# Moving the softplus and du arithmetic of a selective-scan kernel from VectorE to ScalarE and GpSimd

## The chip, the cores and the metric

The kernel runs on one core of a Trainium2 chip. The metric is the device time of one launch in microseconds. Five engines work side by side: TensorE (PE; its weight loads are the track PEld), VectorE (DVE), ScalarE (ACT), GpSimd (POOL) and SyncE (SP). Each runs its own instruction list strictly in order; semaphores tie them together.

## What is computed

The input is 16 sequences ("rows") of 512 tokens by 256 features. Each row passes a Mamba-like layer and then a three-layer feed-forward network (FFN), each with a residual and a layer norm. The piece that matters here, cut from the reference, with 512 channels and 16 states:

```
xx = silu(conv1d(x @ in_w.T))                       # u, [channel, time]
delta = softplus(dt @ dt_w.T + dt_b)
dA  = exp(delta * A);  dBu = delta * B * u
carry = dA * carry + dBu;  y = sum_n carry * C      # scan over time, 16 states
y = (y + u * D) * silu(res)
x = layernorm(x + y @ out_w.T); x = layernorm(x + ffn(x))
```

The kernel builds softplus from pieces. With p the pre-activation including its bias, softplus(p) = max(p, 0) + log(1 + exp(-|p|)), plus a correction for what is lost when 1 is added in float32 (the tile that the code keeps in `du` and subtracts).

## The kernel before

**Layout.** Channels lie on partitions, four chunks of 128 (index `c`, `DC` = 4), and time along the free dimension, 512 elements. So "128x512" is one chunk of one row. The scan has 64 tiles per row (16 states by 4 chunks), taken in 32 pairs of 128x1024.

**Pipeline.** One iteration has 64 steps `s`. In it the kernel scans one row, prepares the next one ("front"), finishes the attention part and FFN of the row before ("tail"), and ends the FFN of the one before that ("end"). Every engine walks through the same 64 steps, and tables at the top of the file (`HALF_AT`, `GELU_AT`, `F_DT`, ...) say in which step each piece is issued. The order of each engine is thus written out by hand. An instruction that waits holds up everything behind it on its engine.

**The scan in the steps.** In even steps TensorE transposes a pair of `dB` tiles into `scan_ps` (L367, `b_pair`), for the pair after next but one, once VectorE has emptied those banks. VectorE scans a pair in an even step (L782) and multiplies by C in an odd step into `hC` (L792). GpSimd issues the DMA that adds `hC` to `y2` in odd steps (L968, `y_pair`). `hC` has two buffers: the multiply of pair p waits until the DMA of pair p-2 has landed. ScalarE makes `dA` (L607) and `dB` (L616), several steps ahead.

**The FFN in the steps.** TensorE does half of a hidden tile in each step of `HALF_AT` (L479); steps 51 to 53 have none. ScalarE applies Gelu (L688) and rounds to the high part (L697); GpSimd subtracts for the low part (L990). The half tile of step 55 needs the low parts that GpSimd makes in step 53.

**The stage that is changed**, in the front, for each chunk c:

1. TensorE, steps 41 to 44 (`F_DT`): the pre-activation into `misc_ps` (L423). The matmul of chunk c+1 waits for `dt_ready` of chunk c, since there is one `misc_ps`.
2. VectorE, a step later: adds the bias, `misc_ps` to `delta2` (L818).
3. ScalarE: Abs into `du` (L650), Exp of the negative (L652).
4. VectorE: 1 + e into a work tile `sp_w` (named out_st or gate in the trace, L829), the lost part into `du` (L831), then max(p,0) minus the lost part (L837).
5. ScalarE, step 51: four Ln (L656), with a table load ahead.
6. VectorE, steps 54 and 55: the sum delta (four L843) and du = u * delta (four L848).
7. TensorE, steps 56 to 59 (`F_DU`): transposes `du` into `misc_ps` (L367); the first waits for all four chunks (`du_ready`). ScalarE copies each out (L662), and the next row's `dB` is made from that.
8. VectorE, steps 57 to 60: y2 = D * u (L854), which the first `y_pair` of the next row waits for.

Of the kernel before, what the change touches and what calls it, by code (L numbers as in the profile page):

```python
# [78 lines left out]
F_DT, F_EXP, F_PLUS, F_MAX, F_LN = (41, 42, 43, 44), (43, 44, 45, 48), (44, 45, 46, 49), (45, 46, 47, 50), 51  # L79
F_DELTA, F_DELTA_U, F_Y, F_DU = (54, 54, 55, 55), (54, 54, 55, 55), (57, 58, 59, 60), (56, 57, 58, 59)  # L80
# [14 lines left out]
def build(nc, x, in_wT, chan, xproj_wT, dt_wT, out_wT, ffn_w, ffn_s, w3_s, ident_in, out):  # L95
# [3 lines left out]
    with ExitStack() as ctx:  # L99
# [93 lines left out]
        sp_lost, sp_ln, sp_max = sem("sp_lost"), sem("sp_ln"), sem("sp_max")  # L193
# [387 lines left out]
        def _(act):  # L581
# [37 lines left out]
            def front_step(r, par, s, end):  # L619
# [135 lines left out]
        def _(dve):  # L755
# [40 lines left out]
            def front_step(r, par, s, tail):  # L796
# [36 lines left out]
                for c in range(DC):  # L833
                    if F_MAX[c] != s:
                        continue
                    dve.wait_ge(sp_lost, r * DC + (c + 1))
                    nc.vector.scalar_tensor_tensor(out=delta2[:, par, c, :], in0=delta2[:, par, c, :], scalar=0.0,  # L837
                                                   in1=du[:, c, :], op0=ALU.max, op1=ALU.subtract).then_inc(sp_max, 1)
                for c in range(DC):
                    if F_DELTA[c] == s:  # L840
                        dve.wait_ge(sp_max, r * DC + (c + 1))
                        dve.wait_ge(sp_ln, r * DC + (c + 1))
                        nc.vector.tensor_tensor(delta2[:, par, c, :], delta2[:, par, c, :], sp_w[c], ALU.add  # L843
                                                ).then_inc(delta_ready, 1)
                for c in range(DC):
                    if F_DELTA_U[c] == s:
                        dve.wait_ge(delta_ready, r * DC + (c + 1))
                        nc.vector.tensor_tensor(du[:, c, :], y2[:, par, c, :], delta2[:, par, c, :], ALU.mult  # L848
                                                ).then_inc(du_ready, 1)
                for c in range(DC):  # L850
                    if F_Y[c] != s:
                        continue
                    dve.wait_ge(du_ready, r * DC + (c + 1))
                    nc.vector.tensor_scalar(y2[:, par, c, :], y2[:, par, c, :], ch[:, c, C_D:C_D + 1], None,  # L854
                                            ALU.mult).then_inc(y_init, 1)
# [101 lines left out]
        def _(pool):  # L957
# [11 lines left out]

            def gate_tile(r, par, c):  # L970
# [100 lines left out]
```

## Time and profile before

| what | value |
|---|---|
| median of 3 runs | 3149.71 us (3144.48 to 3151.66) |
| the profiled execution, its time | 3155.72 us |
| its span, first to last instruction | 3153.9 us |
| mean granted TensorE clock | 0.897 |
| TensorE busy | 2583.1 us (82%) |
| VectorE busy | 2621.1 us (83%) |
| ScalarE busy | 2343.3 us (74%) |
| GpSimd busy | 1071.0 us (34%) |

Three engines are busy for three quarters of the span or more. Such a table doesn't say which of them sets the pace in a given stretch: this is read from the chain of waits, which follows the last instruction back through whatever released each step. Times in the traces are microseconds from the start of the span. Line numbers are those of the kernel before. The piece from 1385 to 1568 us is one iteration in the middle; it and its neighbours look alike.

### The profile page before, as it was taken

Reading aid. Unit: us, or ns where it says so; the run is one execution under the profiler, and the core shown is the slowest. Engines: PE = TensorE matmul, PEld = TensorE weight load, DVE = VectorE, ACT = ScalarE, POOL = GpSimd, SP = SyncE. Lnnn points to the kernel's source line nnn. Section 1 sums busy time; section 2 is a strip of 40 time slices with the busy share of each in tenths; the row PEclk is TensorE's granted clock in tenths of the full one; section 3 lists DMA queues with packets and bytes.
Section 4 is the critical chain, followed back from the end, with each engine's and each line's share of the span. In section 5 each row is a group of like instructions: output and inputs, shape, how many; then the busy total and the mean of one; then the engine's idle time right before and its main releaser. Section 6 shows DMA issues by size and latency. Waiting matters only on the chain.

```text
span 3153.9 us, 41504 instructions
## 1 busy us (share of the span) xinstructions
PE 2583.1 (82%) x12290; PEld 1944.8 (62%) x12290; DVE 2621.1 (83%) x2625; ACT 2343.3 (74%) x3653; POOL 1071.0 (34%) x1028
## 2 busy tenths in 40 slices
PE   4355788888888888988888898888888889898888
PEld 1223566676666666676666766666676756666666
DVE  3678998989898897989889898988989898998830
ACT  2776687877969787796968779697877969687822
POOL 0112333333433433343343334234333423423432
PEclk8566899999989999999989999899999989899999
DMA  1996787787878778787887878787787878778933
GB/s 52 290 321 140 167 193 180 185 197 184 194 179 193 190 181 186 183 194 183 190 188 179 194 181 194 179 196 189 178 190 181 200 186 196 189 180 191 229 111 110
DMA packets 230192, 585.49 MB, mean 186 GB/s; under 512 B 26016, under 2 KB 26400, under 8 KB 229808
## 3 DMA queue, kind: packets, MB, share of 16 engines
q0 software_dynamic: 73728, 268.47, 46.2%
q1 hardware_dynamic: 119344, 246.86, 22.4%
q10 hardware_dynamic: 36864, 67.13, 7.9%
q8 instruction: 115, 1.88, 0.2%
q14 instruction: 141, 1.16, 0.1%
HBM read 281.93 MB, written 31.98 MB: 100 GB/s over the span
## 4 chain that ended last, share of the span: by engine, by line
PE 32%; DVE 29%; ACT 17%; issue 14%; DMA 4%; ACTq 1%; DVEq 1%; SPq 1%; POOL 1%; POOLq 0%
PE ffn_ps L479 17%; DVE scan_ps L782 11%; DVE hC L792 5%; PE scan_ps L367 5%; ACT dB L616 4%; ACT dA L607 3%; DVE y L806 3%; PE misc_ps L372 3%; DMA x<-ffn_w 3%; PE misc_ps L423 2%; DVE gate L899 2%; PE misc_ps L460 2%; PE misc_ps L408 2%; ACT L607 2%; PE misc_ps L367 2%
## 5 line engine op out<-in xcount | busy, mean ns | idle before, releaser
L782 DVE TENSOR_TENSOR_SCAN scan_ps<-dA,scan_ps 128x1024 f32<-128x1024 f32 x512 | 1170.8, 2287 | 57.0 <-PE scan_ps L367 33.2
L968 POOL DMA_DIRECT2D y<-hC x512 | 446.1, 871 | 1811.2 <-DVE hC L792 1735.1
L367 PE MATMUL scan_ps<-ident,dB 128*128 128x128 f32 x4096 | 613.4, 300 | 375.7 <-DVE hC L792 292.3
L367 PEld LDWEIGHTS scan_ps<-ident,dB 128*128 128x128 f32 x4096 | 519.9, 154 | 521.2 <-DVE hC L792 305.5
L616 ACT ACTIVATE dB<-duT,bT 128x512 f32<-128x512 f32 x1024 | 726.4, 711 | 154.5 <-PE scan_ps L367 153.2
L607 ACT ACTIVATE dA<-delta,a_neg 128x512 f32<-128x512 f32 (+1 forms) x1024 | 710.1, 712 | 41.1 <-DVE hC L792 38.0
L479 PE MATMUL ffn_ps<-hb_hi,ring 128*128 128x512 f32 x1536 | 660.1, 430 | 18.4 <-DVE gate L899 8.7
L792 DVE TENSOR_TENSOR hC<-scan_ps,c_rows_sb 128x1024 f32<-128x1024 f32 x512 | 623.6, 1218 | 49.8 <-DMA y<-hC 41.5
L479 PE MATMUL ffn_ps<-hb_lo,ring 128*128 128x512 f32 x1536 | 620.7, 404 | 0.0
L479 PE MATMUL ffn_ps<-ha_hi,ring 128*128 128x512 f32 x1024 | 443.5, 433 | 2.4 <-POOL ha_lo L990 2.4
L479 PE MATMUL ffn_ps<-ha_lo,ring 128*128 128x512 f32 x1024 | 407.7, 398 | 0.0
L990 POOL TENSOR_TENSOR ha_lo<-x,ha_hi 128x512 fp32r<-128x512 f32 x256 | 356.0, 1492 | 89.8 <-ACT ha_hi L697 52.8
L479 PEld LDWEIGHTS ffn_ps<-hb_hi,ring 128*128 128x128 f32 x1536 | 304.6, 198 | 108.4 <-DVE gate L899 29.6
L479 PEld LDWEIGHTS ffn_ps<-hb_lo,ring 128*128 128x128 f32 x1536 | 303.4, 198 | 64.2 <-issue 7.4
L372 PE MATMUL misc_ps<-out_st,inw 128*128 128x512 f32 x512 | 282.3, 679 | 27.5 <-DVE y L806 25.5
L479 PEld LDWEIGHTS ffn_ps<-ha_hi,ring 128*128 128x128 f32 x1024 | 197.8, 193 | 94.9 <-issue 55.5
L479 PEld LDWEIGHTS ffn_ps<-ha_lo,ring 128*128 128x128 f32 x1024 | 197.8, 193 | 48.9 <-issue 12.8
L688 ACT ACTIVATE x<-ffn_ps,fs 128x512 f32<-128x512 f32 x256 | 166.9, 685 | 72.1 <-PE ffn_ps L479 69.7
L990 POOL TENSOR_TENSOR hb_lo<-x,hb_hi 128x512 fp32r<-128x512 f32 x128 | 194.3, 1570 | 33.2 <-ACT hb_hi L697 33.0
L705 ACT ACTIVATE gate<-ffn_ps,s_half 128x512 f32<-128x512 f32 x128 | 87.7, 685 | 116.0 <-PE ffn_ps L479 116.0
L372 PEld LDWEIGHTS misc_ps<-out_st,inw 128*128 128x128 f32 x512 | 100.6, 216 | 115.9 <-issue 74.3
L806 DVE SCALAR_TENSOR_TENSOR y<-misc_ps,conv_half,y 128x511 f32<-128x511 f32 (+2 forms) x192 | 143.3, 747 | 31.0 <-ACT y L630 26.5
(90 smaller groups left out, 2941.9 us busy)
## 6 DMA issues: line engine op xcount, KB each, us to landing
y<-hC POOLq DMA_DIRECT2D x512, 512.0 KB, 5.8
ring<-split_weights SPq DMA_DIRECT2D x704, 256.0 KB, 4.3
c_rows_sb<-c_rows ACTq DMA_DIRECT2D x256, 256.0 KB, 4.0
xt<-x_tok SPq DMA_DIRECT2D x32, 512.0 KB, 6.1
x<-ffn_w SPq DMA_DIRECT2D x22, 512.0 KB, 9.7
split_weights<-ha_hi SPq DMA_DIRECT2D x22, 512.0 KB, 5.2
split_weights<-ha_lo SPq DMA_DIRECT2D x22, 512.0 KB, 7.0
out_tok<-out_st SPq DMA_DIRECT2D x16, 512.0 KB, 2.9
```

The costliest lines, as they stand in the source:

```text
L367: mm = nc.tensor.transpose(dst[:, j * P:(j + 1) * P], src(j), ident[:])
L372: mm = nc.tensor.matmul(misc_ps[:], inw[:, k, col * P:(col + 1) * P], xT[:, k, :], start=(k == 0), stop=(k == KD - 1))
L479: mm = nc.tensor.matmul(dst, w, a, start=(first and n == 0), stop=(last and n == len(steps) - 1))
L607: nc.scalar.activation(dA[:, s % DA_RING, s % 2:], delta2[:, par, c, s % 2:], ACT.Exp, scale=a_neg[:, c, n:n + 1]).then_inc(dA_ready, 1)
L616: nc.scalar.activation(dB[:, n % 2, t, :], duT[:, t, :], ACT.Copy, scale=bT2[:, par, t, n:n + 1]).then_inc(dB_ready, 1)
L688: nc.scalar.activation(x32[:, i % X32, :], ffn_ps[(2 * HC + i) % 3][:], ACT.Gelu, scale=fs[:, 2 + i // HC, i % HC:i % HC + 1]).then_inc(ge ...
L705: nc.scalar.activation(gate[:, o % 2, :], ffn_ps[2 * o % 3][:], ACT.Tanh, scale=s1_half[:, o:o + 1]).then_inc(l1_tanh, 1)
L782: nc.vector.tensor_tensor_scan(b, dA[:, a:a + 2, :].rearrange("p a l -> p (a l)"), b, 0.0, ALU.mult, ALU.add).then_inc(scan_done, 1)
L792: nc.vector.tensor_tensor(hC[:, p % 2], scan_ps[:, h:h + 2, :], c_rows[:, n % 2].unsqueeze(1).to_broadcast([P, 2, SEQ]), ALU.mult).then_in ...
L806: nc.vector.scalar_tensor_tensor(out=y2[:, par, c, back:], in0=misc_ps[:, 0:SEQ - back], scalar=conv_half[:, c, tap:tap + 1], in1=y2[:, pa ...
L968: pool.dma_start(y2[:, par, c:c + 2, :], hC[:, p % 2], accum_op=ALU.add).then_inc(y_added[p % 2], 16)
L990: nc.gpsimd.tensor_tensor(lo[:, i % HC, :], x32[:, i % X32, :], hi[:, i % HC, :].bitcast(F32), ALU.subtract).then_inc(ffn_lo, 1)
```

## The change

The additions of the bias leave VectorE. ScalarE reads the pre-activation from PSUM twice, as Abs with bias and as Relu with bias, one step after the matmul. The second read frees `misc_ps`. VectorE keeps only the 1 + e and the lost part, one step earlier. Everything behind them goes to GpSimd in a new `front_step`: Relu minus the lost part (steps 44, 45, 46, 49), plus the logarithm (steps 52 and 53), times u (steps 53 and 54) and D * u (steps 57 to 60).

```
-F_DT, F_EXP, F_PLUS, F_MAX, F_LN = (41, 42, 43, 44), (43, 44, 45, 48), (44, 45, 46, 49), (45, 46, 47, 50), 51
-F_DELTA, F_DELTA_U, F_Y, F_DU = (54, 54, 55, 55), (54, 54, 55, 55), (57, 58, 59, 60), (56, 57, 58, 59)
+F_DT, F_PLUS, F_SUB, F_LN = (41, 42, 43, 44), (43, 44, 45, 48), (44, 45, 46, 49), 51
+F_DELTA, F_DELTA_U, F_Y, F_DU = (52, 52, 53, 53), (53, 53, 54, 54), (57, 58, 59, 60), (56, 57, 58, 59)

 ScalarE, front_step:
-                for c in range(DC):
-                    if F_EXP[c] != s:
-                        continue
-                    act.wait_ge(dt_ready, r * DC + (c + 1))
-                    nc.scalar.activation(du[:, c, :], delta2[:, par, c, :], ACT.Abs).then_inc(sp_abs, 1)
+                if s - 1 in F_DT:
+                    c = F_DT.index(s - 1)
+                    act.wait_ge(pe_dt, r * DC + (c + 1))
+                    nc.scalar.activation(du[:, c, :], misc_ps[:], ACT.Abs, bias=ch[:, c, C_DTB:C_DTB + 1]
+                                         ).then_inc(sp_abs, 1)
+                    nc.scalar.activation(delta2[:, par, c, :], misc_ps[:], ACT.Relu, bias=ch[:, c, C_DTB:C_DTB + 1]
+                                         ).then_inc(dt_ready, 1)

 VectorE, front_step: without L818, L837, L843, L848 and L854
-                    nc.vector.tensor_scalar(delta2[:, par, c, :], misc_ps[:], ch[:, c, C_DTB:C_DTB + 1], None,
-                                            ALU.add).then_inc(dt_ready, 1)
...
-                        nc.vector.tensor_tensor(du[:, c, :], y2[:, par, c, :], delta2[:, par, c, :], ALU.mult
-                                                ).then_inc(du_ready, 1)
...

 GpSimd, new, called in each step behind y_pair and the low parts:
+            def front_step(r, par, s):
+                for c in range(DC):
+                    if F_SUB[c] == s:
+                        pool.wait_ge(dt_ready, r * DC + (c + 1))
+                        pool.wait_ge(sp_lost, r * DC + (c + 1))
+                        nc.gpsimd.tensor_tensor(delta2[:, par, c, :], delta2[:, par, c, :], du[:, c, :], ALU.subtract
+                                                ).then_inc(sp_base, 1)
+                for c in range(DC):
+                    if F_DELTA[c] == s:
+                        pool.wait_ge(sp_base, r * DC + (c + 1))
+                        pool.wait_ge(sp_ln, r * DC + (c + 1))
+                        nc.gpsimd.tensor_tensor(delta2[:, par, c, :], delta2[:, par, c, :], sp_w[c], ALU.add
+                                                ).then_inc(delta_ready, 1)
+                for c in range(DC):
+                    if F_DELTA_U[c] == s:
+                        pool.wait_ge(u_ready, r * DC + (c + 1))
+                        pool.wait_ge(delta_ready, r * DC + (c + 1))
+                        nc.gpsimd.tensor_tensor(du[:, c, :], y2[:, par, c, :], delta2[:, par, c, :], ALU.mult
+                                                ).then_inc(du_ready, 1)
+                for c in range(DC):
+                    if F_Y[c] == s:
+                        pool.wait_ge(pe_dbl, r + 1)
+                        pool.wait_ge(du_ready, r * DC + (c + 1))
+                        nc.gpsimd.tensor_tensor(y2[:, par, c, :], y2[:, par, c, :],
+                                                ch[:, c, C_D:C_D + 1].to_broadcast([P, SEQ]), ALU.mult
+                                                ).then_inc(y_init, 1)
```

GpSimd from step 51 to step 57, before (the low parts of tiles 6 and 7 of the second FFN layer between two `y_pair` DMAs):

```order
L968 DMA y<-hC 128x1024 [waits hC_done,y_added1]
L961 REGISTER_ALU
L965 REGISTER_ALU [waits hC_done]
L968 DMA y<-hC 128x1024 [waits y_added0]
L988 REGISTER_ALU
L990 TENSOR_TENSOR hb_lo<-x,hb_hi 128x512 [waits ffn_hi]
L988 REGISTER_ALU
L990 TENSOR_TENSOR hb_lo<-x,hb_hi 128x512 [waits ffn_hi]
L961 REGISTER_ALU
L968 DMA y<-hC 128x1024 [waits hC_done,y_added1]
```

The same place in the changed kernel (its line 942 is L968, its line 991 is L990):

```order
L942 DMA y<-hC 128x1024 [waits hC_done,y_added1]
L955 TENSOR_TENSOR delta<-delta,out_st 128x512 [waits sp_ln,sp_base]
L955 TENSOR_TENSOR delta<-delta,gate 128x512 [waits sp_ln,sp_base]
...
L942 DMA y<-hC 128x1024 [waits y_added0]
...
L991 TENSOR_TENSOR hb_lo<-x,hb_hi 128x512 [waits ffn_hi]
L989 REGISTER_ALU
L991 TENSOR_TENSOR hb_lo<-x,hb_hi 128x512 [waits ffn_hi]
L955 TENSOR_TENSOR delta<-delta,gate 128x512 [waits sp_ln,sp_base]
L955 TENSOR_TENSOR delta<-delta,out_st 128x512 [waits sp_ln,sp_base]
L961 TENSOR_TENSOR du<-y,delta 128x512 [waits delta_ready,u_ready] x4
L935 REGISTER_ALU
L942 DMA y<-hC 128x1024 [waits hC_done,y_added1]
```

Two delta sums now stand ahead of the DMA of step 53 and the two low parts, and two sums and all four products behind them. The DMA of step 55 comes last.

VectorE from step 52 to step 55, before:

```order
L782 SCALAR_TENSOR_TENSOR scan_ps<-dA,scan_ps 128x1024 [waits pe_dBu,dA_ready]
L792 TENSOR_TENSOR hC<-scan_ps,c_rows_sb 128x1024 [waits scan_done,y_added0,c_loaded1]
L782 SCALAR_TENSOR_TENSOR scan_ps<-dA,scan_ps 128x1024 [waits pe_dBu,dA_ready]
L843 TENSOR_TENSOR delta<-delta,out_st 128x512 [waits sp_ln,sp_max]
L843 TENSOR_TENSOR delta<-delta,gate 128x512 [waits sp_ln,sp_max]
L848 TENSOR_TENSOR du<-y,delta 128x512 [waits delta_ready] x2
L792 TENSOR_TENSOR hC<-scan_ps,c_rows_sb 128x1024 [waits scan_done,y_added1]
```

In the changed kernel:

```order
L784 SCALAR_TENSOR_TENSOR scan_ps<-dA,scan_ps 128x1024 [waits pe_dBu,dA_ready]
L794 TENSOR_TENSOR hC<-scan_ps,c_rows_sb 128x1024 [waits scan_done,y_added0,c_loaded1]
L784 SCALAR_TENSOR_TENSOR scan_ps<-dA,scan_ps 128x1024 [waits pe_dBu,dA_ready]
L794 TENSOR_TENSOR hC<-scan_ps,c_rows_sb 128x1024 [waits scan_done,y_added1]
```

Only scans and multiplies by C are left there.

## Rows read from the trace of the kernel before

**Rows 1.** By stretch, busy PE, PEld, DVE, ACT, POOL; then clock, DMA share, GB/s.
```profile
1425.00:1498.00 73.00, 57.93 (x272) 43.18 (x270) 70.11 (x87) 46.37 (x75) 22.25 (x23) 0.91 0.77 185
1498.00:1532.00 34.00, 33.58 (x152) 22.77 (x152) 29.79 (x29) 30.82 (x50) 12.53 (x12) 1.00 0.78 187
1532.00:1548.00 16.00, 8.55 (x41) 7.07 (x41) 15.97 (x15) 14.43 (x21) 6.60 (x6) 0.79 0.73 159
1548.00:1590.00 42.00, 39.94 (x204) 31.45 (x205) 32.65 (x24) 39.25 (x60) 17.89 (x17) 1.00 0.93 215
```

**Rows 2.** The chain that ended last, 1530 to 1612: start, us, what.
```profile
1532.48 1.28 ACT L688
...
1536.96 0.55 ACT gate L656
...
1539.85 2.26 DVE delta L843 x2
...
1547.25 0.69 DVE du L848
...
1547.99 0.66 PE misc_ps L367 x4
...
1566.99 1.68 issue
...
1590.37 0.89 PE scan_ps L367 x8
```

**Rows 3.** Timeline of ScalarE, 1495 to 1570: start, us, instruction, idle before.
```profile
1508.71 0.61 ACT L650 ACTIVATE du<-delta 128x512 f32<-128x512 f32 x1
...
1515.88 0.72 ACT L616 ACTIVATE dB<-duT,bT 128x512 f32<-128x512 f32 x1 [1.65 <-PE scan_ps L367]
...
1536.35 0.63 ACT L656 ACTIVATE out_st<-out_st 128x512 f32<-128x512 f32 x1
```

**Rows 4.** PE's waits over the whole span: us, times, longest.
```profile
PE misc_ps L367 <- DVE du L848: 25.6, 16, 8.7
```

**Rows 5.** Groups by line and shape, VectorE: busy, mean ns, idle before.
```profile
L837 DVE SCALAR_TENSOR_TENSOR delta<-delta,du 128x512 f32<-128x512 f32 x64 | 54.7, 857 | 0.0
L848 DVE TENSOR_TENSOR du<-y,delta 128x512 f32<-128x512 f32 x64 | 53.0, 868 | 0.0
L818 DVE TENSOR_SCALAR delta<-misc_ps,ch 128x512 f32<-128x512 f32 x64 | 48.0, 750 | 65.3 <-PE misc_ps L423 63.3
L843 DVE TENSOR_TENSOR delta<-delta,gate 128x512 f32<-128x512 f32 x32 | 36.8, 1151 | 0.0
L854 DVE TENSOR_SCALAR y<-y,ch 128x512 f32<-128x512 f32 x64 | 29.9, 471 | 0.0
L843 DVE TENSOR_TENSOR delta<-delta,out_st 128x512 f32<-128x512 f32 x32 | 24.1, 752 | 0.0
```

**Rows 6.** GpSimd's L975 and L968: duration ns min/median/max, first and last start.
```profile
L975 POOL TENSOR_TENSOR y<-y,gate x64: 1260/1572/1622, 304.7 to 3027.2; 128x512 f32<-128x512 f32 x64
L968 POOL DMA_DIRECT2D y<-hC x512: 850/870/1052, 89.3 to 3003.3; - x171
```

**Rows 7.** Timeline of GpSimd: one after another at 1583, two at 1539.75.
```profile
1539.75 3.49 POOL L990 TENSOR_TENSOR hb_lo<-x,hb_hi 128x512 fp32r<-128x512 f32 x2 [0.59 <-ACT hb_hi L697]
...
1583.09 1.56 POOL L975 TENSOR_TENSOR y<-y,gate 128x512 f32<-128x512 f32 x1
1584.34 1.54 POOL L990 TENSOR_TENSOR ha_lo<-x,ha_hi 128x512 fp32r<-128x512 f32 x1
```

**Rows 8.** Timeline of VectorE at 1540.35, while GpSimd's two low parts run.
```profile
1540.35 1.76 DVE L843 TENSOR_TENSOR delta<-delta,gate 128x512 f32<-128x512 f32 x1
```

**Rows 9.** The stretch 1537 to 1543: columns as in rows 1.
```profile
1537.00:1543.00 6.00, 3.72 (x13) 3.34 (x14) 6.00 (x5) 5.97 (x10) 4.11 (x3) 0.50 0.91 187
```

**Rows 10.** The page's DMA issues: KB each, us from issue to landing.
```profile
y<-hC POOLq DMA_DIRECT2D x512, 512.0 KB, 5.8
```

**Rows 11.** Timeline of VectorE: the first scan of the next iteration.
```profile
1568.02 2.30 DVE L782 TENSOR_TENSOR_SCAN scan_ps<-dA,scan_ps 128x1024 f32<-128x1024 f32 x1 [4.13 <-issue]
```

More of the change, by code:

```diff
@@ L192, in build @@
         dt_ready, sp_abs, sp_exp, sp_plus = sem("dt_ready"), sem("sp_abs"), sem("sp_exp"), sem("sp_plus")
-        sp_lost, sp_ln, sp_max = sem("sp_lost"), sem("sp_ln"), sem("sp_max")
+        sp_lost, sp_ln, sp_base = sem("sp_lost"), sem("sp_ln"), sem("sp_base")
         delta_ready, du_ready, y_init = sem("delta_ready"), sem("du_ready"), sem("y_init")
@@ L814, in front_step @@
                                                    ).then_inc(u_ready, 1)
-                if s - 1 in F_DT:
-                    c = F_DT.index(s - 1)
-                    dve.wait_ge(pe_dt, r * DC + (c + 1))
-                    nc.vector.tensor_scalar(delta2[:, par, c, :], misc_ps[:], ch[:, c, C_DTB:C_DTB + 1], None,
-                                            ALU.add).then_inc(dt_ready, 1)
                 for c in range(DC):
@@ L832, in front_step @@
                                                    op0=ALU.subtract, op1=ALU.subtract).then_inc(sp_lost, 1)
[L833 to L847, printed above, removed]
-                        nc.vector.tensor_tensor(du[:, c, :], y2[:, par, c, :], delta2[:, par, c, :], ALU.mult
-                                                ).then_inc(du_ready, 1)
[L850 to L855, printed above, removed]
             def statistics(which, src, r, half, ready):
@@ L1013, in iteration @@
                         ffn_step(end, s + TILES)
+                    if front is not None:
+                        front_step(front, fpar, s)
             iteration(-1, 1)
```

## The prediction, written before the changed kernel ran

> **What bounds the kernel now.** I cut one iteration into stretches first and then read the chain of waits through the same piece. Busy shares alone mislead here, because the pace changes hands. From 1425 to 1498 VectorE is busy 70.1 of 73 us, so it sets the pace. From 1498 to 1532 TensorE is busy 33.6 of 34, and from 1548 to 1590 it is busy 39.9 of 42 [rows 1]. The changed stage begins in the second of these stretches (steps 39 to 50). Its end lies in the piece between, 1532 to 1548, where TensorE works only 8.6 of 16 us.
>
> The chain says what that piece waits for [rows 2]. ScalarE starts a Gelu at 1532.48 when TensorE's last half tile is done, then loads a table and takes the four logarithms. VectorE makes the sums (L843) and products (L848) behind its scan, the last from 1547.25. TensorE's transpose of du starts at 1547.99, and from there it is TensorE until 1590 almost without a gap. The first logarithm ends at 1536.35 + 0.63 = 1536.98 [rows 3]. So the path has 10.96 us from there to du complete at 1547.25 + 0.69 = 1547.94. TensorE already waits for it: 25.6 us in 16 waits, 1.6 us per row of input [rows 4]. This path decides the change, and it ends in step 56.
>
> **What leaves VectorE.** Per row of input, over 16 rows: 48.0 + 54.7 + (36.8 + 24.1) + 53.0 + 29.9 = 246.5 us, or 15.4 us each [rows 5]. That is 8% of the span, on the engine with the most work. But only the eight sums and products lie on the path. The bias additions stand in the stretch where VectorE itself waited 63.3 us for the matmul (the L818 row) and TensorE sets the pace, and the D products (L854) stand beside TensorE's full stretch. VectorE is free again when the next iteration begins: it idles 4.13 us before its first scan [rows 11]. In the stretch that VectorE bounds, nothing is removed. So of 15.4 us nothing but the sums and products can pay, and they pay only if GpSimd is quicker.
>
> **What GpSimd now takes, on the path.** From the first logarithm it must issue, in this order: two sums, the DMA of step 53, two low parts of the FFN, two sums, four products. These are ten element-wise instructions and one DMA. Its element-wise instruction reads 1.26 at least and 1.57 at the median [rows 6]. The longer readings overlap their neighbour: two that stand one after another start 1.25 apart although each reads 1.55 [rows 7]. I take 1.26, since this is what a queue of ten costs, and 1.57 as the upper end. The DMA issue costs 0.87 [rows 6]. With 0.2 for the hand-over from ScalarE (an estimate), that is 10 x 1.26 + 0.87 + 0.2 = 13.7 us, so du is complete at 1550.7 instead of 1547.94: 2.7 us later. At 1.57 it is 16.8 us, 5.8 later. Below 1.26 no row speaks for it, and the break-even is (10.96 - 0.87 - 0.2) / 10 = 0.99 us per instruction.
>
> Contention won't lengthen these ten. Before, a sum on VectorE took 1.76 instead of about 0.75 (the mean of the out_st sums, rows 5) while the low parts ran, and two low parts took 3.49 together instead of 2 x 1.26 [rows 7, 8]. That was two engines on one path, and it is already in the 10.96. Now VectorE has only scans and multiplies in these steps, each with one operand in PSUM. The Trainium skill, SBUF — State Buffer, "Who interferes with whom", states the same as a lock: a VectorE instruction with two SBUF inputs and a GpSimd one that reads SBUF exclude each other for their whole length. Rows 8 agree. By it the four Relu-minus-lost subtractions may collide with VectorE's lost parts in steps 44 to 48, but that is where TensorE sets the pace.
>
> The low parts keep their time. The half tile of step 55 needed them at 1543.2 (1539.75 + 3.49). Now they are issued behind two sums and the DMA, at 1540.6 to 1543.1. So TensorE reaches step 56 as before and waits there 1.6 + 2.7 = about 4 us.
>
> **What TensorE's clock adds.** After the short stop at 1532 the granted clock was 0.50 (1.2 GHz) from 1537 to 1543, and 1.00 on both sides [rows 1, 9]. TensorE had been nearly idle before it fell. A stop of 4 us in step 56 may bring a second such episode, between nothing and some 2 us of lost time. I take 0.8.
>
> **What ScalarE takes.** Four more reads of about 0.61 [rows 3], 2.4 us per row of input, and Abs and Exp of each chunk one step earlier. The last pair moves from step 48 to step 45, ahead of the Gelus of step 46. ScalarE idles 1.65 us at 1515.88 for TensorE, and by step 49 it is where it was. But the second read, and not VectorE's addition, now frees `misc_ps`. In the old order ScalarE comes to chunk 0 only at 1508.71 [rows 3], one step later than now; moved up by that step and read twice, the bank is free at about the same time (an estimate), which is just when the next matmul of the chain wants it. I take 0.2 us per row of input for the four, from 0 to 1.5.
>
> **The queues behind it.** The DMA of step 53 waits behind two sums, and that of step 55 behind all ten. It is issued at 1550.7 and lands 5.8 later [rows 10], at 1556.5. VectorE's multiply of step 59 waits for it, as hC has two buffers. So VectorE will show a wait for y<-hC of several us per row of input. Before, it reached the end of the iteration 4.13 us ahead of its next scan [rows 11], and TensorE now comes some 4 us later still. A delay of 2 to 3 us in step 59 is covered by that; without the cover it would cost those 2 to 3 us per row of input once more.
>
> **The sum.** Per row of input 2.7 + 0.8 + 0.2 = 3.7 us. Nothing takes it back, since TensorE works on end to end and VectorE comes next with its own full stretch. Fifteen rows: 55. The first row of input is prepared before any scan: eight instructions of 1.26 instead of about 0.75 on the bare path, 4 us. Together 59, near enough +60. The profiled execution (3155.7, of which the span is 3153.9) would come to 3216. The median of the runs stood 6 us below it, at 3149.7, so I predict 3210.
>
> **Rivals.** (1) *The queue costs more.* GpSimd's instructions take 1.57 each in a row, and the clock falls every time (2 us): 5.8 + 2 - 1 for VectorE's lead = 6.8 x 15 + 4 = +106, 3256. For it: the median in rows 6. Against it: the 1.25 pitch in rows 7. (2) *Slack behind the path takes part.* TensorE stands still 1.68 us at the loop's end (rows 2, 1566.99), and after 1590 ScalarE and VectorE share the chain. If 2 us of 3.7 vanish there: 1.7 x 15 + 4 = +30, 3180. Against it: that stop is issue time, which moves along. (3) *Faster.* VectorE's relief pays and GpSimd is off the path. It decides where the ten instructions take less than about 0.86 us each, so that du is there when TensorE arrives, and saves the 1.6 us wait of rows 4 in 15 rows: -24, 3126. No row of GpSimd is under 1.26. (4) *No difference*, if they take just under 1 us: 3150. A price from the Trainium skill for this: GPSIMD Engine Reference, "Elementwise — side-by-side cycle accounting", gives about 2.6 cycles per element, 1.11 us for 512 at its 1.2 GHz (an estimate), and by it the sum would be 2.7 - 1.5 = 1.2 us on the path and about +38 in all; the 1.26 of rows 6 is this kernel's own and stands. The same page advises against plain element-wise work on this engine, about twice VectorE's time, and 1.26 against 0.75 agrees.
>
> **Chances.** Forecast 0.56, (1) 0.16, (2) 0.14, (3) 0.08, (4) 0.06. Faster by over 0.2% (about 6 us, what a measurement of this kernel can tell from no change) is (3): 0.08. Within it is (4): 0.06. Slower is the rest, 0.86. The range takes in (1) and (2): 3168 to 3262.
>
> **What would show it.** Right: GpSimd's ten instructions without idle time between the first logarithm and the DMA of step 55, 13 to 14 us from that logarithm to the end of the last product; TensorE's L367 waiting for GpSimd's du, some 4 us in each of 15 rows of input; VectorE about 240 us less busy yet more idle, with a large wait for y<-hC; GpSimd up by about 320 us (16 x 16 x 1.26). Wrong: TensorE's wait for du no longer than now, GpSimd's instructions shorter than 1 us, or the matmuls of L423 held up by ScalarE's reads by more than a microsecond per row of input.

## The result, and the profile after

| | before | changed |
|---|---|---|
| median, us | 3150.68 (4 runs, 3144.48 to 3155.80) | 3196.97 (4 runs, 3195.78 to 3198.21) |
| span of the profiled execution, us | 3153.9 | 3196.4 |
| mean granted TensorE clock | 0.897 | 0.894 |

The changed kernel is 46 us slower: ratio 1.0151, interval 1.0135 to 1.0167. The prediction said 3210 and slower, so 60 us where 46 were measured. One of the five runs of e2_scalar_part below was a slow one, at 8535.82 us, and its median is taken over the other four.

Page of the changed kernel, busy time of each engine:

```profile
PE 2597.0 (81%) x12290; PEld 1958.2 (61%) x12290; DVE 2430.4 (76%) x2305; ACT 2372.4 (74%) x3717; POOL 1362.4 (43%) x1284
```

VectorE has 191 us less and GpSimd 291 us more. The most loaded engine was relieved by 6% of the span, and the kernel got slower.

Waits of the changed kernel over the whole span, the answer to [rows 4] (who waits for whom: us, times, longest):

```profile
DVE scan_ps L784 <- PE scan_ps L367: 149.2, 105, 23.2
...
DVE hC L794 <- DMA y<-hC: 130.9, 88, 6.1
...
PE misc_ps L367 <- POOL du L961: 63.0, 16, 12.5
```

TensorE now waits 63.0 us for du, from GpSimd, where it waited 25.6 for VectorE. The longest of these waits, 12.5 us now and 8.7 before, falls on the first row of input; the other 15 come to 3.4 us each now and 1.1 before. VectorE's relief has turned into waits: 130.9 us for the DMAs of `hC` (41.5 before), and more for TensorE (149.2 against 33.2).

GpSimd of the changed kernel, its timeline in one iteration, the answer to [rows 7]. The first logarithm ended at 1553.97.

```profile
1554.13 1.26 POOL L955 TENSOR_TENSOR delta<-delta,out_st 128x512 f32<-128x512 f32 x1 [3.00 <-ACT out_st L658]
1555.36 1.27 POOL L955 TENSOR_TENSOR delta<-delta,gate 128x512 f32<-128x512 f32 x1
1556.58 0.84 POOL L942 DMA_DIRECT2D y<-hC  x1
1557.19 2.77 POOL L991 TENSOR_TENSOR hb_lo<-x,hb_hi 128x512 fp32r<-128x512 f32 x2
1559.67 1.52 POOL L955 TENSOR_TENSOR delta<-delta,gate 128x512 f32<-128x512 f32 x1
1560.90 1.53 POOL L955 TENSOR_TENSOR delta<-delta,out_st 128x512 f32<-128x512 f32 x1
1562.14 5.18 POOL L961 TENSOR_TENSOR du<-y,delta 128x512 f32<-128x512 f32 x4
1567.05 2.01 POOL L942 DMA_DIRECT2D y<-hC  x2
```

The ten instructions and the DMA stand without a gap, 13.35 us from the logarithm to the last product's end at 1567.32. Starts of neighbours lie 1.23 us apart, also where a reading says 1.52: the longer readings overlap. VectorE in the same stretch, the answer to [rows 8]:

```profile
1559.25 2.29 DVE L784 TENSOR_TENSOR_SCAN scan_ps<-dA,scan_ps 128x1024 f32<-128x1024 f32 x1 [2.87 <-ACT dA L607]
...
1564.59 2.29 DVE L784 TENSOR_TENSOR_SCAN scan_ps<-dA,scan_ps 128x1024 f32<-128x1024 f32 x1 [1.79 <-PE scan_ps L367]
1571.98 1.22 DVE L794 TENSOR_TENSOR hC<-scan_ps,c_rows_sb 128x1024 f32<-128x1024 f32 x1 [5.10 <-DMA y<-hC]
```

VectorE idles 2.87, 1.79 and 5.10 us in the piece where it used to make the sums. Nothing it could do there was left to it.

The iteration by stretch, the answer to [rows 1] (columns as there), with four short stretches around TensorE's stop for du:

```profile
1442.00:1515.00 73.00, 58.16 (x272) 42.89 (x271) 69.89 (x87) 45.97 (x75) 22.26 (x23) 0.91 0.79 186
1515.00:1549.00 34.00, 33.59 (x153) 22.90 (x153) 29.35 (x23) 32.98 (x54) 16.81 (x16) 1.00 0.82 191
1549.00:1568.00 19.00, 9.97 (x47) 8.24 (x46) 12.09 (x7) 14.42 (x21) 16.00 (x16) 0.82 0.63 149
...
1561.80:1564.40 2.60, 2.60 (x16) 2.07 (x14) 1.00 (x1) 1.71 (x3) 2.60 (x3) 1.00 0.40 119
1564.40:1567.40 3.00, 0.10 (x2) 0.02 (x1) 2.29 (x1) 0.00 (x0) 3.00 (x4) 1.00 0.27 90
1568.50:1571.50 3.00, 3.00 (x12) 2.36 (x10) 0.00 (x0) 1.47 (x3) 2.63 (x3) 0.52 1.03 194
1567.40:1568.50 1.10, 1.10 (x7) 1.01 (x8) 0.00 (x0) 0.35 (x1) 1.10 (x3) 1.00 0.00 0
...
1574.00:1612.00 38.00, 36.05 (x187) 28.21 (x186) 25.76 (x17) 35.94 (x55) 19.54 (x18) 1.00 0.88 208
```

The first two stretches are what they were. The piece in which TensorE waits has grown from 16 to 19 us, and the clock falls a second time: it is 1.00 while TensorE still works (1561.8 to 1564.4), while it stands and in its first microsecond of work (1567.4 to 1568.5), and 0.52 over 1568.5 to 1571.5. In the 13 iterations of the table below the fall comes between 0.5 us ahead of TensorE's first transpose of du, in the stop still, and 1.2 us behind it. Before, it was 1.00 over the whole of that stretch.

### The profile page after: what moved, and what is told of

It reads as the page before. It is cut to its first block, busy times and chain, and to the rows that moved or that the text cites. A ratio compares the mean times of both kernels' runs of the same rounds, so it can differ in the third digit from the quotient of the medians.

```text
span 3196.4 us, 41749 instructions
## 1 busy us (share of the span) xinstructions
PE 2597.0 (81%) x12290; PEld 1958.2 (61%) x12290; DVE 2430.4 (76%) x2305; ACT 2372.4 (74%) x3717; POOL 1362.4 (43%) x1284
## 4 chain that ended last, share of the span: by engine, by line
ACT 26%; DVE 25%; PE 23%; issue 17%; DMA 4%; POOL 3%; ACTq 1%; DVEq 1%; SPq 0%; POOLq 0%
PE ffn_ps L479 11%; DVE scan_ps L784 9%; ACT dB L616 6%; DVE hC L794 5%; ACT dA L607 5%; DVE y L808 3%; PE scan_ps L367 3%; PE misc_ps L372 3%; DMA x<-ffn_w 2%; PE misc_ps L408 2%; ACT x L690 2%; ACT L690 2%; DVE gate L873 2%; ACT L607 2%; PE misc_ps L367 2%
## 5 line engine op out<-in xcount | busy, mean ns | idle before, releaser
L784 DVE TENSOR_TENSOR_SCAN scan_ps<-dA,scan_ps 128x1024 f32<-128x1024 f32 x512 | 1171.2, 2288 | 213.2 <-PE scan_ps L367 149.2
L942 POOL DMA_DIRECT2D y<-hC x512 | 455.1, 905 | 1377.5 <-DVE hC L794 1317.2
L794 DVE TENSOR_TENSOR hC<-scan_ps,c_rows_sb 128x1024 f32<-128x1024 f32 x512 | 624.0, 1219 | 141.9 <-DMA y<-hC 130.9
L479 PE MATMUL ffn_ps<-hb_hi,ring 128*128 128x512 f32 x1536 | 670.7, 437 | 20.3 <-DVE gate L873 10.5
L479 PE MATMUL ffn_ps<-hb_lo,ring 128*128 128x512 f32 x1536 | 628.4, 409 | 0.0
L991 POOL TENSOR_TENSOR hb_lo<-x,hb_hi 128x512 fp32r<-128x512 f32 x128 | 185.4, 1493 | 48.9 <-ACT hb_hi L699 48.7
```

The lines of the kernel that those rows point to most:

```text
L479: mm = nc.tensor.matmul(dst, w, a, start=(first and n == 0), stop=(last and n == len(steps) - 1))
L784: nc.vector.tensor_tensor_scan(b, dA[:, a:a + 2, :].rearrange("p a l -> p (a l)"), b, 0.0, ALU.mult, ALU.add).then_inc(scan_done, 1)
L794: nc.vector.tensor_tensor(hC[:, p % 2], scan_ps[:, h:h + 2, :], c_rows[:, n % 2].unsqueeze(1).to_broadcast([P, 2, SEQ]), ALU.mult).then_in ...
L942: pool.dma_start(y2[:, par, c:c + 2, :], hC[:, p % 2], accum_op=ALU.add).then_inc(y_added[p % 2], 16)
L991: nc.gpsimd.tensor_tensor(lo[:, i % HC, :], x32[:, i % X32, :], hi[:, i % HC, :].bitcast(F32), ALU.subtract).then_inc(ffn_lo, 1)
```

## The experiments

To place each gain and loss I cut the iteration at instructions of TensorE and took the mean over rows of input 2 to 14, counted from 0 (13 iterations), from the start and end times in each trace. "Path" is from the end of the first logarithm to the end of the last product; "du taken" is from that logarithm to TensorE's first transpose of du; "stop" is TensorE's idle time right ahead of its first transpose of du; "56 to 61" is from that transpose to the next row's first transpose of the input; "ScalarE" is from the first matmul of step 45 to the first logarithm's end. Microseconds:

| kernel | path | du taken | stop | 56 to 61 | ScalarE | whole iteration |
|---|---|---|---|---|---|---|
| before | 10.98 | 11.03 | 1.19 | 10.97 | 18.11 | 182.93 |
| changed | 13.37 | 13.42 | 3.33 | 12.48 | 17.73 | 185.99 |
| e1_sums_back | 7.71 | 9.75 | none | 10.91 | 17.73 | 181.04 |
| e2_scalar_part | 8.01 | 9.93 | none | 10.92 | 17.73 | 181.33 |
| e3_du_scale_part | 10.96 | 11.02 | 1.11 | 10.97 | 18.11 | 182.35 |
| e4_two_more | 16.07 | 16.12 | 6.19 | 12.86 | 17.74 | 188.98 |
| e5_products_back | 11.37 | 11.42 | 0.10 | 10.96 | 17.73 | 182.30 |
| e6_half_tile_early | 8.20 | 10.76 | none | 10.91 | 17.73 | 181.84 |
| e7_low_on_vector | 10.88 | 17.34 | none | 10.94 | 17.73 | 188.10 |
| e8_chain_alone | 13.37 | 13.43 | 3.47 | 12.53 | 18.11 | 186.32 |
| e9_logs_later | 7.12 | 7.17 | 1.31 | 10.97 | 19.38 | 180.51 |
| e10_both | 7.09 | 7.15 | 0.99 | 11.12 | 19.38 | 180.27 |

All the rest of the iteration takes 142.1 to 143.0 us in each of them. In e11 and e12 below, which only add a tail to the kernel before, its iteration takes 182.60 and 182.86, so a few tenths in the last column mean nothing. The kernel before stood at a median of 3149.43 (e1 to e4), 3149.17 (e5 to e8), 3148.21 (e9 to e11) and 3147.91 (e12).

**e1_sums_back**, against the changed kernel: sums and products on VectorE again, in their old steps.

```
-F_DELTA, F_DELTA_U, ... = (52, 52, 53, 53), (53, 53, 54, 54), ...
+F_DELTA, F_DELTA_U, ... = (54, 54, 55, 55), (54, 54, 55, 55), ...
 (L955 and L961 from GpSimd to VectorE's front_step, as in the kernel before)
```

> The changed kernel with the four sums and four products of each row of input back on VectorE in steps 54 and 55; ScalarE's Abs and Relu, the subtractions and D*u on GpSimd stay. Theory A (the cost is GpSimd's chain of ten instructions between the first logarithm and du, 13.4 us against 10.96): du is ready 9 to 10 us after the first logarithm, TensorE waits for it no more than before, and the time is 3130 to 3152. Rival B (ScalarE's second PSUM read, or GpSimd's other eight instructions, cost most of the 46 us): 3175 to 3195.

Measured: 3128.86, ratio to before 0.9933 (0.9920 to 0.9945), a microsecond under the 3130 to 3152 expected. So the sums and products on GpSimd cost 68 us, and what is left of the change gains 21.

**e2_scalar_part**, against the kernel before: only ScalarE's part. Its two reads replace the bias addition, and VectorE subtracts (L834) a step earlier than it took max and subtracted (L837). All else stays on VectorE.

```
-F_DT, F_EXP, F_PLUS, F_MAX, F_LN = ..., (45, 46, 47, 50), 51
+F_DT, F_PLUS, F_SUB, F_LN = ..., (44, 45, 46, 49), 51
+  nc.scalar.activation(du, misc_ps, ACT.Abs, bias=...)
+  nc.scalar.activation(delta2, misc_ps, ACT.Relu, bias=...)
-  nc.vector.tensor_scalar(delta2, misc_ps, bias, None, ALU.add)
-  nc.vector.scalar_tensor_tensor(delta2, delta2, 0.0, du, max, subtract)
+  nc.vector.tensor_tensor(delta2, delta2, du, ALU.subtract)
```

> The kernel before with ScalarE's part of the change alone (Abs and Relu with bias from PSUM, one step earlier); all that stands behind it stays on VectorE, as subtraction instead of max and subtraction. Theory A: 3145 to 3156, TensorE's L423 held up by no more than 0.3 us per row of input. Rival B: if freeing the PSUM bank through ScalarE is what costs, at least 15 us more than before, 3165 or above.

Measured: 3124.72, ratio 0.9919 (0.9905 to 0.9933): a miss, the gain is 25 us where I had expected 3145 to 3156. Its VectorE, one iteration (the first logarithm ended at 1523.85):

```profile
1522.68 2.29 DVE L784 TENSOR_TENSOR_SCAN scan_ps<-dA,scan_ps 128x1024 f32<-128x1024 f32 x1
1524.88 0.67 DVE L840 TENSOR_TENSOR delta<-delta,out_st 128x512 f32<-128x512 f32 x1
...
1526.06 2.38 DVE L845 TENSOR_TENSOR du<-y,delta 128x512 f32<-128x512 f32 x2
...
1530.70 1.28 DVE L845 TENSOR_TENSOR du<-y,delta 128x512 f32<-128x512 f32 x2
```

And that of the kernel before in the same place (the first logarithm ended at 1536.98):

```profile
1531.57 1.48 DVE L837 SCALAR_TENSOR_TENSOR delta<-delta,du 128x512 f32<-128x512 f32 x1
...
1537.56 2.28 DVE L782 TENSOR_TENSOR_SCAN scan_ps<-dA,scan_ps 128x1024 f32<-128x1024 f32 x1
1539.76 0.67 DVE L843 TENSOR_TENSOR delta<-delta,out_st 128x512 f32<-128x512 f32 x1
...
1542.02 2.37 DVE L848 TENSOR_TENSOR du<-y,delta 128x512 f32<-128x512 f32 x2
```

Before, the first sum began 2.8 us behind the first logarithm: VectorE was still at its scan. The 1.48 us of the last L837 stood ahead of the multiply, the scan and so the sums. In e2 the sum begins 1.0 us behind the logarithm. Over the 13 iterations the sums begin 1.9 us earlier, of which L837's turn of 1.4 is the greater part, and sums and products last 1.0 us less: before, a sum of 1.76 [rows 8] and a pair of products of 2.37 met GpSimd's two low parts, in e2 only the pair of 2.38 did. TensorE no longer waits for du (7.7 us in 2 waits for L845). The path is 3.0 us shorter, but TensorE takes du only 1.1 us earlier, since it now waits for ScalarE's dB ahead of its last half tile: 88.0 us in 15 waits, 63.2 in 17 before. The whole iteration is 1.60 us shorter: 1.10 of it is du taken earlier, 0.38 ScalarE's stretch. Times 15 that is 24 us.

**e3_du_scale_part**, against the kernel before: only D * u on GpSimd.

```
-  nc.vector.tensor_scalar(y2, y2, D, None, ALU.mult)
+  nc.gpsimd.tensor_tensor(y2, y2, D.to_broadcast([P, SEQ]), ALU.mult)
```

> The kernel before with D*u alone moved to GpSimd (steps 57 to 60). VectorE loses 1.9 us per row of input beside TensorE's full stretch. Theory A: no difference, 3144 to 3156. Rival C (delayed y<-hC DMAs hold up VectorE and then TensorE): 3160 or above.

Measured: 3149.93, ratio 0.9997 (0.9988 to 1.0007). It costs and gains nothing.

**e4_two_more**, against the changed kernel: the products of the first two chunks made twice, two more GpSimd instructions on the path.

```
+  if c < 2:
+      nc.gpsimd.tensor_tensor(du, y2, delta2, ALU.mult).then_inc(du_twice, 1)
+      pool.wait_ge(du_twice, r * 2 + (c + 1))
   nc.gpsimd.tensor_tensor(du, y2, delta2, ALU.mult).then_inc(du_ready, 1)
```

> The changed kernel with two of the four products made twice on GpSimd, so two more instructions in the chain. Theory A (the chain has no slack): 2 x 1.26 = 2.5 us more per row of input from logarithm to du, 35 to 42 us more than the changed kernel, 3232 to 3240. Rival C (part is swallowed behind the path): 3210 to 3225. If GpSimd isn't on the path: 3197.

Measured: 3246.41, ratio 1.0311 (1.0297 to 1.0324), 49 us over the changed kernel; I had expected 35 to 42. The path grew by 2.70 (each added pair of instruction and wait 1.35) and the iteration by 2.99: nothing behind the path takes up a delay.

**e8_chain_alone**, against the kernel before: only sums and products go to GpSimd, in the steps of the changed kernel.

```
-F_DELTA, F_DELTA_U, ... = (54, 54, 55, 55), (54, 54, 55, 55), ...
+F_DELTA, F_DELTA_U, ... = (52, 52, 53, 53), (53, 53, 54, 54), ...
 (L843 and L848 from VectorE to GpSimd)
```

> The kernel before with the sums and products alone moved to GpSimd, as in the change; bias, max, Abs and D*u stay where they were. Theory A: path 13.4 us, TensorE stops for about 3.3 us in step 56, second fall of the clock; the change's time and what ScalarE's part gives besides the path (0.4 us per row of input) on top: 3197 to 3210. Rival B (the chain costs only together with the other moved parts): 3175 or below.

Measured: 3202.76, ratio 1.0172 (1.0157 to 1.0188), 54 us. Path, stop and steps 56 to 61 are those of the changed kernel. With e2 and e3 the account of the change closes: 54 for the chain, and ScalarE's part gives back at most a little of it, 6 us by the medians (3202.76 - 3196.97), with intervals that overlap. That is less than its own 25: with GpSimd on the path VectorE's early finish has no taker, and by the table only the shorter ScalarE stretch is left, 0.38 us in 15 rows.

**e5_products_back**, against the changed kernel: the products on VectorE (steps 54 and 55), the sums on GpSimd.

```
-F_DELTA_U = (53, 53, 54, 54)
+F_DELTA_U = (54, 54, 55, 55)
-  nc.gpsimd.tensor_tensor(du, y2, delta2, ALU.mult)
+  nc.vector.tensor_tensor(du, y2, delta2, ALU.mult)
```

> The changed kernel with the four products back on VectorE (steps 54, 55); the four sums stay on GpSimd (steps 52, 53). Theory A with the floor that e1 and e2 showed (TensorE comes to step 56 some 9.8 us after the first logarithm): the last sum is ready 8.8 us after it, the products end at about 10.2, no long stop of TensorE and so no second fall of the clock; 3128 to 3142. If GpSimd's sums cost in proportion to their number (half of the 68 us between e1 and the changed kernel): about 3163.

Measured: 3148.24, ratio 0.9998 (0.9988 to 1.0008), 6 us above the 3128 to 3142 that I had expected. Timelines of its VectorE and its GpSimd, the same piece:

```profile
1531.25 7.58 DVE L833 TENSOR_TENSOR du<-y,delta 128x512 f32<-128x512 f32 x2 [1.02 <-POOL delta L960]
```

```profile
1531.19 1.26 POOL L960 TENSOR_TENSOR delta<-delta,gate 128x512 f32<-128x512 f32 x1
1532.40 0.85 POOL L947 DMA_DIRECT2D y<-hC  x1
1533.01 2.77 POOL L990 TENSOR_TENSOR hb_lo<-x,hb_hi 128x512 fp32r<-128x512 f32 x2
1535.48 1.54 POOL L960 TENSOR_TENSOR delta<-delta,gate 128x512 f32<-128x512 f32 x1
1536.72 1.55 POOL L960 TENSOR_TENSOR delta<-delta,out_st 128x512 f32<-128x512 f32 x1
```

Two products took 7.58 us, where two of them alone take 1.27: the first 1.75, the second, from 1532.93, 5.90. They end at 1538.83, half a microsecond after GpSimd's run of four (1536.72 + 1.55 = 1538.27).

**e7_low_on_vector**, against the changed kernel: the two low parts of step 53 on VectorE, so that GpSimd's path has eight instructions.

```
+  def low_step(f, s):                     (VectorE)
+      if s == 53:
+          for i in (6, 7):
+              nc.vector.tensor_tensor(hb_lo, x32, hb_hi, ALU.subtract)
```

> The changed kernel with the two low parts of step 53 on VectorE instead of GpSimd: eight instructions and one DMA in the chain. Theory A: the path falls from 13.4 by 2 x 1.26 to about 10.9 us, TensorE waits about 1 us for du, the clock doesn't fall again; 3135 to 3150. Rival D (VectorE's two-input subtractions lock GpSimd's sums out, so that nothing is won): 3170 to 3195.

Measured: 3229.97, ratio 1.0251 (1.0236 to 1.0266), far from the 3135 to 3150 expected. The path fell to 10.88 as worked out, yet another wait took its place. VectorE, GpSimd and a wait of it:

```profile
1565.68 9.42 DVE L889 TENSOR_TENSOR hb_lo<-x,hb_hi 128x512 fp32r<-128x512 f32 x2 [4.42 <-ACT hb_hi L699]
```

```profile
1565.48 0.84 POOL L951 DMA_DIRECT2D y<-hC  x1
1566.09 1.54 POOL L964 TENSOR_TENSOR delta<-delta,gate 128x512 f32<-128x512 f32 x1
1567.32 1.54 POOL L964 TENSOR_TENSOR delta<-delta,out_st 128x512 f32<-128x512 f32 x1
1568.57 5.18 POOL L970 TENSOR_TENSOR du<-y,delta 128x512 f32<-128x512 f32 x4
```

```profile
PE ffn_ps L479 <- DVE hb_lo L889: 69.7, 15, 5.3
```

VectorE's two subtractions took 9.42 us. The first took 8.63 of them, to 1574.31, half a microsecond after GpSimd's run of six (1568.57 + 5.18 = 1573.75); the second, with GpSimd at rest, took 0.69. TensorE's half tile waited for them instead of for du, and its granted clock was 0.64 over 1565 to 1577, with TensorE busy 6.90 of 12 us.

**e6_half_tile_early**, against e2: TensorE's half tile of step 54 in step 53, so that TensorE has work while du is made.

```
-           54, 55, 56, 57, ...   (HALF_AT)
+           53, 55, 56, 57, ...
```

> e2 (ScalarE's part alone) with TensorE's half tile of step 54 moved up to step 53, ahead of the scan transposes that wait for ScalarE's dB. If TensorE's own work from there sets the 9.8 us floor, the path falls by 0.5 to 1.5 us per row of input and the granted clock stays up longer: 3095 to 3118. If the low parts of step 53 set it: no difference, 3122 to 3130.

Measured: 3140.67, ratio 0.9968 (0.9957 to 0.9979), 16 us worse than e2 and not better, a miss. TensorE now comes to the half tile before its low parts are made and waits for those, 36.9 us in 16 waits (2.1 in one wait in e2), while its waits for dB fall from 88.0 to 62.6:

```profile
1530.41 1.96 PE L367 MATMUL scan_ps<-ident,dB 128*128 128x128 f32 x8 [4.25 <-ACT dB L616]
1534.48 0.79 PE L479 MATMUL ffn_ps<-hb_hi,ring 128*128 128x512 f32 x1 [2.10 <-POOL hb_lo L987]
```

**e9_logs_later and e10_both**, against e2: the logarithms a step later (`F_LN` 52); and the same with e6's half tile.

```
-F_LN = 51
+F_LN = 52
```

> e2 (ScalarE's part alone) with the four logarithms in step 52 instead of 51, behind the dB and the two high parts of step 52. dB, the high parts and so the low parts come 2.9 us earlier on ScalarE (table load and four logarithms), the logarithms about 1.8 us later. If TensorE's stop for dB (6 us per row of input) sets the floor of 9.8 us that e2 has, du becomes the last thing again and 0.3 to 1.2 us per row of input are won: 3105 to 3122. If the logarithms' delay decides: 3135 to 3155.

> e9 with the half tile of step 54 moved to step 53, as in e6. With the low parts ready early there is nothing for TensorE to wait for but du: e9's time within 6 us, 3100 to 3122. If e6's loss came from the moved half tile itself and not from the late low parts, 10 us or more above e9.

Measured: 3123.61, ratio 0.9915 (0.9897 to 0.9933), and 3124.30, ratio 0.9927 (0.9909 to 0.9945), both 2 us above the range expected. In e9 the waits for dB fall to 8.6 us, the path to 7.12 and du is taken at 7.17, while the stretch ahead of it grows by 1.65. e10 stays within a microsecond of e9, so the moved half tile by itself doesn't cost what e6 lost. But in e10 too TensorE waits for the low parts, 45.5 us in 16 waits, and isn't slower for it; what e6 lost is not settled by these runs. The intervals of e2, e9 and e10 overlap; e9 has the lowest median, and whether it beats e2 stays open. All three beat both kernels.

**e11_lock and e12_lock_after_dma**, the kernel before with a tail that makes nothing of use: in each of four phases GpSimd runs eight subtractions, and VectorE issues one instruction behind the first of them. In e12 phases 2 to 4 put GpSimd's `y` DMA ahead of the eight.

```
+  for ph in range(4):                                  (GpSimd)
+      pool.wait_ge(lk_dve, ph + 1)
+      if ph: pool.dma_start(y2, hC, accum_op=ALU.add)      (e12 only)
+      for i in range(8):
+          if ph == 2 and i: pool.wait_ge(lk_pool, ...)    (spaced)
+          nc.gpsimd.tensor_tensor(ha_lo, x32, ha_hi, ALU.subtract)
```

> The kernel before with a tail behind its last store, four phases of eight GpSimd subtractions of 128x512, during which VectorE gets one instruction, released by GpSimd's first: phase 0 a product with two SBUF inputs, phase 1 a multiply with one input in PSUM, phase 2 the product again but with each GpSimd instruction waiting for the one before it, phase 3 an addition of a constant. Theory L (a VectorE instruction with two SBUF inputs is locked out for the whole back-to-back run of GpSimd): phase 0 takes 7 to 9.5 us, phase 1 1.2 us, phase 2 about 2 us, since GpSimd's queue runs empty between two instructions. Rival M (locked out for one GpSimd instruction only): phase 0 at most 2.2 us and like phase 2. Phase 3 is open: 0.42 us if it never waits.

> As the run with the tail before it, other phases of eight GpSimd subtractions with one VectorE instruction released by the first: phase 0 no DMA issue ahead, VectorE product with two SBUF inputs; phase 1 a DMA issue by GpSimd directly ahead of the eight, same product; phase 2 the same, each GpSimd instruction also waiting for the one before; phase 3 a DMA issue ahead, VectorE multiply with one input in PSUM. Theory L2 (behind a DMA issue GpSimd's instructions read 1.54 us and overlap, and such a run keeps VectorE's two-input instruction out until it ends): phase 0 1.7 us as before, phase 1 7 to 9.5 us, phase 2 under 3 us, phase 3 1.2 us. Rival M (one GpSimd instruction at most, and the 8.6 us of e7 had another cause): phases 0, 1 and 2 all under 2.5 us.

VectorE of e11, its four phases (two SBUF inputs; one in PSUM; two SBUF inputs with GpSimd spaced by waits; one SBUF input with a constant):

```profile
3150.32 1.73 DVE L967 TENSOR_TENSOR du<-y,delta 128x512 f32<-128x512 f32 x1 [1.38 <-POOL ha_lo L1039]
3160.71 1.22 DVE L961 TENSOR_TENSOR hC<-scan_ps,c_rows_sb 128x1024 f32<-128x1024 f32 x1 [8.66 <-POOL ha_lo L1039]
3170.60 1.78 DVE L967 TENSOR_TENSOR du<-y,delta 128x512 f32<-128x512 f32 x1 [8.66 <-POOL ha_lo L1039]
3181.65 1.40 DVE L965 TENSOR_SCALAR gate<-du 128x512 f32<-128x512 f32 x1 [9.27 <-POOL ha_lo L1039]
```

VectorE and GpSimd of e12 (no DMA ahead; a DMA ahead; a DMA ahead, GpSimd spaced; a DMA ahead, VectorE reading PSUM):

```profile
3154.87 1.73 DVE L965 TENSOR_TENSOR du<-y,delta 128x512 f32<-128x512 f32 x1 [1.37 <-POOL ha_lo L1039]
3166.43 8.95 DVE L965 TENSOR_TENSOR du<-y,delta 128x512 f32<-128x512 f32 x1 [9.83 <-POOL ha_lo L1039]
3178.26 1.78 DVE L965 TENSOR_TENSOR du<-y,delta 128x512 f32<-128x512 f32 x1 [2.87 <-POOL ha_lo L1039]
3190.44 1.23 DVE L961 TENSOR_TENSOR hC<-scan_ps,c_rows_sb 128x1024 f32<-128x1024 f32 x1 [10.40 <-POOL ha_lo L1039]
```

```profile
3153.57 10.25 POOL L1039 TENSOR_TENSOR ha_lo<-x,ha_hi 128x512 fp32r<-128x512 f32 x8 [6.39 <-DVE du L957]
3164.11 0.92 POOL L1035 DMA_DIRECT2D y<-hC  x1 [0.30 <-POOL ha_lo L1039]
3164.77 10.05 POOL L1039 TENSOR_TENSOR ha_lo<-x,ha_hi 128x512 fp32r<-128x512 f32 x8
```

e11 found no trace of what e5 and e7 had shown: the product waited for about one GpSimd instruction (1.73 against 0.64, half of the 1.28 for two in the kernel before), not eight. e12 found it: with a DMA issue directly ahead, the same product took 8.95 us, to half a microsecond after GpSimd's run (3164.77 + 10.05 = 3174.82). The third phase of e12 had the same DMA on its way and its product took 1.78, so it is the unbroken run behind the issue that holds VectorE out, and not the transfer. Each ran once, but the difference is a factor of five.

## Why the prediction was right, and where it was off

The sign and the mechanism were right. By its own steps, per row of input:

- **The path: 13.7 predicted, 13.37 measured**, a delay of 2.39 instead of 2.7. Ten instructions at 1.26, the DMA and the hand-over came out 0.3 too long: the pitch was 1.23, and the DMA issue, which reads 0.84, held the queue for 0.61 (1556.58 to 1557.19). The upper end, 1.57 each, was the reading of overlapping instructions, and the rival built on it (3256) fell. The Trainium skill's price (GPSIMD Engine Reference, "Elementwise — side-by-side cycle accounting", 1.11 by the estimate in the prediction) lies below the 1.23, and the 38 us by it below the 46. e8 shows this chain alone makes the loss, e1 that without it there is none, e4 that more of it costs more. TensorE's stop was 3.33 and not about 4, since the 1.6 us per row to which the 2.7 was added was misread: of the 25.6 us in rows 4, 8.7 belong to the first row of input, and 1.1 is left for each of the others.
- **"So of 15.4 us nothing but the sums and products can pay": this step failed.** ScalarE's part paid 25 us (e2). I had looked at each removed instruction only in the stretch where it ran. The last L837 ran at 1531.57, at the end of TensorE's full stretch, but stood ahead of VectorE's multiply and scan, and these ahead of the sums. VectorE was late for its part of the path by 2.8 us [rows 2, 3], and that made TensorE wait. Rival (3) had the condition wrong: not GpSimd's speed, but VectorE coming earlier. That its -24 and 3126 lie so near e2's 3124.72 is luck: 1.1 us in 15 rows are 17, and the rest of e2's gain comes mostly from ScalarE's shorter stretch. In the changed kernel VectorE's part of it couldn't pay, as VectorE was off the path. Which of the two, the four bias additions or the earlier subtraction, gives more of it was not taken apart.
- **The clock: 0.8 predicted, 1.5 measured.** Steps 56 to 61 went from 10.97 to 12.48. Counting the episodes of half clock in the traces, there were 65 with 654 us before and 81 with 681 us in the changed kernel; per iteration, steps 56 to 61 had 3.3 us more of it and the rest behind them 2.1 us less. e4 bears on it: with a stop of 6.2 us the stretch took 12.86, so between 3.3 and 6.2 us the price goes little with the stop's length (3.3 us cost 1.5, none or 1.2 us cost nothing).
- **ScalarE's reads: 0.2 cost predicted, 0.38 gained.** Each read took 0.68 where I had put 0.61, but the stretch up to the logarithms fell from 18.11 to 17.73, in e2 as in the changed kernel; that VectorE's addition no longer stands between matmul and Abs is the likely reason, not a tested one. TensorE's wait for the bank (L423) is 7.7 us in 6 waits, against 6.3 in 5 before, so 0.1 us more per row of input.
- **Slack.** 0.46 us went in the rest of the iteration, which had 2.1 us less of half clock (that this is the reason is not shown); rival (2) gave it 2. Together: 2.39 + 1.51 - 0.38 - 0.46 = 3.06 per row, against 3.7; 13 rows make 39.8 of the 42.5 by which the spans differ. The sum is nearer than its terms: the clock 0.7 too low and ScalarE's reads 0.58 too high nearly cancel, which is luck.
- **The first row's 4 us: the term failed.** Its path grew by 5.0, but when the 13 iterations begin (421.1 us, 420.3 before) only 0.8 of it is left; 2.0 more come behind them.
- **The cover behind it held.** VectorE's wait for `y<-hC` rose from 41.5 to 130.9 us, as foreseen, and VectorE still idles ahead of the first scan of the next iteration, now for `dA`. The answer to [rows 11]:

```profile
1588.49 2.30 DVE L784 TENSOR_TENSOR_SCAN scan_ps<-dA,scan_ps 128x1024 f32<-128x1024 f32 x1 [4.76 <-ACT dA L607]
```

- **Busy times: VectorE -191 (240 predicted), GpSimd +291 (320).** The latter is 1.14 per added instruction, as overlapping readings are counted once. VectorE's 191 is 56 short of the 246.5 that its rows add up to. Two groups that stayed there got slower and make 21 of them; overlap makes about 26 (an estimate: 320 instructions that read 0.68 where neighbours start 0.60 apart). Of the two, out_st took 694 in e2 as well, so most of its rise doesn't come from the work moved to GpSimd. By shape, the changed kernel's groups (busy, mean ns | idle before), where L829 and L831 had taken 417 and 692 before:

```profile
L828 DVE SCALAR_TENSOR_TENSOR du<-gate,du 128x512 f32<-128x512 f32 x32 | 32.8, 1025 | 1.1
...
L826 DVE TENSOR_SCALAR out_st<-du 128x512 f32<-128x512 f32 x32 | 23.7, 741 | 43.1 <-ACT du L654 39.4 <-PE misc_ps L414 3.8
```

- **"Contention won't lengthen these ten": held**, and the reason given held too. VectorE's instructions with an operand in PSUM took 1.22 beside GpSimd in e11 and 1.23 in e12, as everywhere. But I had taken the cost of a collision as one instruction's length, and that was luck of the layout: with one product on VectorE, directly behind a DMA issue, it is GpSimd's whole run. The Trainium skill, SBUF — State Buffer, "Who interferes with whom", which the prediction leaned on, has the lock last for a whole instruction. The 1.73 of both tails agrees with that; the 8.95 behind a DMA issue goes beyond one instruction, and there the measurement decides. GpSimd's readings overlap in just that case, so that the lock may never come free between them; no run shows this.

## What to carry to other kernels

Work that leaves the busiest engine pays only through the wait it shortens, so follow what stands behind a removed instruction on its engine up to the next thing others wait for, not only the stretch in which it ran. A chain on the path goes to the engine with the shortest pitch from one instruction to the next, however idle another is: eight element-wise instructions per row of input on GpSimd cost 54 us here, and letting ScalarE, which had room, add the bias, with VectorE's subtraction a step earlier, gained 25. Look at the longest of a group of waits before you divide their sum by the rows: one of 8.7 us made 1.1 per row look like 1.6. Keep products of two SBUF operands on VectorE away from back-to-back runs on GpSimd that follow a DMA issue.

## What the runs showed of the hardware

- Directly behind a DMA issue of GpSimd, its back-to-back instructions of 128x512 read 1.47 to 1.56 us with starts 1.22 to 1.25 apart, so they overlap, and a VectorE instruction with two SBUF inputs doesn't get in between until the last ends: 8.95 us for one against a run of eight (e12), 8.63 against six (e7), 5.90 against four (e5). Without a DMA issue ahead they read 1.26, and with one ahead but a wait on a semaphore between GpSimd's instructions mostly so; VectorE then loses one turn (1.73 and 1.78). Why a DMA issue makes the difference no run shows.
- A constant-operand `tensor_scalar` with one SBUF input is held up as well: 1.40 in e11 against 0.42 alone.
- Around a stop of 2.9 to 3.7 us in the changed kernel TensorE's granted clock fell from 1.00 to 0.50 (2.4 to 1.2 GHz) in each of 13 iterations, between 0.5 us before work began again and 1.2 us after it; steps 56 to 61 had 3.3 us of it and took 1.5 us longer. With the 6.2 us stop of e4 it fell 1.5 to 3.2 us before work began again.
- ScalarE's Abs and Relu from PSUM with a bias per partition took 0.68 us, against 0.61 for Abs from SBUF without one.
